# A graph network's last stages: buffers of their own for the last graph, twelve graphs fetched early, three engines for the final norm

## The reference

```
x1 = layernorm(x + attention(x, adj) @ Wo.T)               # per graph
top1 = argmax(mean_nodes(x1) @ router_w + router_b)        # one expert per graph
out = adj @ (x1 @ expert_w[top1])                          # per graph
mean, var = moments of out over all nodes of all graphs with the same expert
y = relu((out - mean) * rsqrt(var + 1e-5) * gamma[top1] + beta[top1])
result = layernorm(x1 + y)                                 # per graph
```

## Time and profile before

| | |
|---|---|
| median of 3 runs | 2607.61 us (2606.01 to 2607.66) |
| profiled execution | 2607.4 us |
| its span, first to last instruction | 2605.6 us |
| busy: PE, DVE, POOL, ACT | 86%, 69%, 65%, 60% of the span |
| granted TensorE clock, mean | 0.935 of full speed |
| chain that ended last | PE 69%, DVE 14% of the span |
| HBM read, written | 272.25 MB, 67.11 MB |

### The profile page before, as it was taken

One profiled execution on the slowest core, in us unless ns is written; L12 is line 12 of the kernel. 1 busy time (PEld: TensorE's weight loads), 2 busy tenths in 40 slices (PEclk: granted clock), 3 DMA queues, 4 the chain that ended last, 5 costly groups with the idle time before them and its releaser, 6 DMA issues.

```text
span 2605.6 us, 49110 instructions
## 1 busy us (share of the span) xinstructions
PE 2246.6 (86%) x14496; PEld 1732.1 (66%) x14496; DVE 1794.4 (69%) x4607; ACT 1563.0 (60%) x3664; POOL 1700.6 (65%) x3148
## 2 busy tenths in 40 slices
PE   3678898999989898989999898989899998986442
PEld 2456676777767676767777676767677776765332
DVE  2475867767676868677776768586777767674588
ACT  0457666666666666666666666666666666662232
POOL 0678777777777777777777777777777776771000
PEclk7789999999999999999999999999999999998766
DMA  6487474655646474746565564747465564622697
GB/s 216 137 260 236 122 250 123 195 170 183 185 149 199 138 236 128 246 118 197 168 184 181 154 197 136 238 129 245 119 204 161 185 184 153 193 82 97 232 345 246
DMA packets 215346, 476.82 MB, mean 183 GB/s; under 512 B 40944, under 2 KB 49136, under 8 KB 208304
## 3 DMA queue, kind: packets, MB, share of 16 engines
q1 hardware_dynamic: 215088, 473.74, 59.1%
HBM read 272.25 MB, written 67.11 MB: 130 GB/s over the span
## 4 chain that ended last, share of the span: by engine, by line
PE 69%; DVE 14%; issue 5%; POOL 3%; ACT 3%; SPq 3%; DMA 2%; DVEq 0%; ACTq 0%; POOLq 0%
PE t_bank L346 14%; PE p_bank L259 13%; PE p_bank L260 12%; PE p_bank L261 12%; PE o_bank L365 9%; PE s_bank L329 7%; SPq L699 2%; DVE att L493 2%; DVE ln_raw L1051 2%; POOL fold L672 2%; DVE xt L556 1%; DVE x_lo L556 1%; POOL fold L674 1%; PE o_bank L356 1%; ACT att L419 1%
## 5 line engine op out<-in xcount | busy, mean ns | idle before, releaser
L672 POOL TENSOR_TENSOR fold<-att 128x256 f32<-128x256 f32 x1024 | 765.6, 748 | 494.3 <-DVE nmax L493 407.9
L493 DVE CUSTOM_DVE_ANT_0 att<-s_bank,adj_t 128x512 f32<-128x512 f32 x1024 | 695.1, 683 | 383.1 <-PE s_bank L329 382.1
L419 ACT ACTIVATE att<-att,nmax 128x512 f32<-128x512 f32 x1024 | 738.7, 722 | 181.6 <-POOL fold L672 167.7
L467 ACT ACTIVATE pt<-t_bank 128x512 f32<-128x512 f32 x768 | 452.7, 596 | 399.1 <-PE o_bank L365 267.6
L346 PE MATMUL t_bank<-ident,att 128*128 128x128 f32 x4096 | 637.3, 279 | 19.8 <-DVE pt L502 9.5
L346 PEld LDWEIGHTS t_bank<-ident,att 128*128 128x128 f32 x4096 | 506.7, 143 | 206.1 <-issue 76.8
L329 PE MATMUL s_bank<-k_stack,q_stack 128*128 128x512 f32 x1024 | 501.4, 491 | 74.3 <-DVE nmax L493 73.8
L674 POOL TENSOR_TENSOR fold<-fold 128x128 f32<-128x128 f32 x1024 | 499.3, 488 | 80.3
L679 POOL TENSOR_TENSOR fold<-fold 128x64 f32<-128x64 f32 x1024 | 357.3, 349 | 80.2
L329 PEld LDWEIGHTS s_bank<-k_stack,q_stack 128*128 128x128 f32 x1024 | 200.0, 195 | 94.3 <-DVE nmax L493 91.6
L365 PE MATMUL o_bank<-pt,v 128*32 128x256 f32 x4096 | 248.5, 383 | 6.6 <-issue 5.8
(11 more groups left out here) (157 smaller groups left out, 3656.8 us busy)
## 6 DMA issues: line engine op xcount, KB each, us to landing
q_stack<-qk_t SPq DMA_DIRECT2D x1024, 64.0 KB, 3.2
k_stack<-qk_t SPq DMA_DIRECT2D x1024, 64.0 KB, 2.0
qk_w<-qk_split SPq DMA_DIRECT2D x123, 512.0 KB, 4.9
slot_a<-vo_split SPq DMA_DIRECT2D x16, 2048.0 KB, 9.7
slot_a<-expert_split SPq DMA_DIRECT2D x16, 2048.0 KB, 8.1
slot_b<-vo_split SPq DMA_DIRECT2D x15, 2048.0 KB, 8.2
stage<-in_xT SPq DMA_DIRECT2D x16, 1024.0 KB, 5.6
adj_t<-in_adj SPq DMA_DIRECT2D x64, 256.0 KB, 7.7
```

The costliest lines, as they stand in the source:

```text
L419: eng.activation(att[:, u % 4, j, :], att[:, u % 4, j, :], ACT.Exp, bias=nmax[:, u % 4, j:j + 1], scale=-1.0, accum_out=rsum[:, u % 4, j:j ...
L467: eng.activation(pt[:, j, :, (u % 2) * P:(u % 2 + 1) * P], t_bank[r % 2][:, :].rearrange("p (m n) -> p m n", m=NT), ACT.Copy).then_inc(act ...
L493: eng.tensor_tensor_reduce(out=att[:, u % 4, j, :], in0=s_bank[r % 2][:, :], in1=adj_t[:, t, :], scale=-2.0, scalar=3.0e38, op0=ALU.add, o ...
L672: eng.tensor_tensor(fold1[:, :], a[:, 0:256], a[:, 256:512], ALU.add).then_inc(pool_fold1, 1)
```

## The change

Four things, all at the end of the program.

1. SBUF tensors get plain views over the same bytes (`overlaid`), so that every large buffer can be the home of a graph in the last phase.
2. The second layer of graph 15 in TAIL has homes of its own: Wo in q_stack, adjT in xt, x in adj_t, the low half in v. Its loads move into the stage before (slots 10 and 13); ACT rounds adjT in slot 13 and POOL subtracts in slot 14 there. `O-` and `S-` write s_bank and t_bank, four banks. The store of x1 of graph 15 and that of its mixed result go away: both stay in SBUF. Newton's steps become ACT's Sqrt and a reciprocal.
3. The batch norm of all experts is done at once on wide tiles; the count per expert moves behind the router's choice.
4. The last phase has no loop: graph 15 first, then 0 to 14. Graphs 0 to 11 are fetched as buffers come free from slot 9 of graph 15's stage on, 12 to 14 between the stores. POOL applies scale and shift of channels 2 and 3, ACT those of 0 and 1 with relu; DVE's add also takes the maximum with 0 and sums the row; ACT squares the deviations and sums them; DVE normalises three tiles and POOL the fourth.

In the order of the pieces: the banks, `dve_rstd`, SP's two new parts, POOL's two functions of the last phase, ACT's, and DVE's adds before and after.

```diff
+        def bank_at(b, task):
+            if b == B and task[0] in ("O-", "S-"):
+                return (s_bank + t_bank)[task[1]]
+            return p_bank[bank_of[task]]
...
+            if b == B:
+                eng.wait_ge(act_std, 2)
+                eng.reciprocal(ln_rstd, ln_std).then_inc(dve_newton, 1)
...
+        def sp_last(eng, b, u):
+            if u == 9:
...
+                fetch(eng, 0)
+            if u == 10:
+                wait(eng, dve_mean, b, 1, 0)
+                wait(eng, pool_at, b, NT, 0)
+                eng.dma_start(stage[:, :, :], adjT[b].rearrange("(t p) n -> p t n", p=P)).then_inc(ld_at, 16)
+            if u == 13:
+                wait(eng, pe["score"], b, STEPS, STEPS)
+                eng.dma_start(q_stack[:].bitcast(F32), vo_dram[1]).then_inc(ld_wo, 16)
+                wait(eng, dve_logit, b, STEPS, STEPS)
+                eng.dma_start(adj_t[:, :, :], x[b].rearrange("(t p) n -> p t n", p=P)).then_inc(ld_x, 16)
+                fetch(eng, 1)
...
+            if u == 14:
+                wait(eng, pe["S"], b, NT, 0)
+                fetch(eng, 2)
+        def sp_tail(eng, b, u):
+            if u == 0:
+                wait(eng, pe["turn"], b, STEPS, 0)
+                fetch(eng, 3)
+                fetch(eng, 4)
+                wait(eng, pe["pv"], b, PAIRS, 0)
+                fetch(eng, 5)
+            if u == 5:
+                wait(eng, pe["O"], b, NT, 0)
+                fetch(eng, 6)
+                fetch(eng, 7)
...
+            def affine(n):
...
+                for t in POOL_CHANNELS:
+                    pool.tensor_scalar(y_home[i][:, t, :], y_home[i][:, t, :], g_affine[:, i, t, 0:1],
+                                       g_affine[:, i, t, 1:2], ALU.mult, ALU.add).then_inc(pool_affine, 1)
+            def normed(n):
+                z = z_home[OUT_ORDER[n]]
+                pool.wait_ge(dve_frstd, n + 1)
+                for t in POOL_ROWS:
+                    pool.tensor_scalar(z[:, t, :], z[:, t, :], f_mean[:, n % 2, t:t + 1], f_rstd[:, n % 2, t:t + 1],
+                                       ALU.add, ALU.mult).then_inc(pool_out, 1)
+            for n in range(B):
+                if n + 2 < B:
+                    affine(n + 2)
+                normed(n)
...
+            def deviation(n):
...
+                for t in range(NT):
+                    act.activation(y_home[i][:, t, :], z_home[i][:, t, :], ACT.Square, bias=f_mean[:, n % 2, t:t + 1],
+                                   accum_out=f_var[:, n % 2, t:t + 1]).then_inc(act_square, 1)
...
-                        dve.tensor_tensor(z[:, t, :], back_bank[(NT * i + t) % 8][:, :], z[:, t, :],
-                                          ALU.add).then_inc(dve_res, 1)
...
-                        dve.bn_stats(ln_raw[:, t, :], z[:, t, :]).then_inc(dve_fln, 1)
...
-                        dve.bn_aggr(ln_mv[:, t, :], ln_raw[:, t, :]).then_inc(dve_fln, 1)
...
+                    dve.scalar_tensor_tensor(out=z[:, t, :], in0=back_bank[(NT * n + t) % 8][:, :], scalar=0.0,
+                                             in1=z[:, t, :], op0=ALU.max, op1=ALU.add,
+                                             accum_out=f_sum[:, n % 2, t:t + 1]).then_inc(dve_res, 1)
...
+            residual(0)
+            for n in range(B):
+                if n + 1 < B:
+                    residual(n + 1)
+                normed(n)
```

More of the change, by code:

```diff
@@ L441, in act_slot @@
             for j in range(HG):
+                if (u, j) == (2, 0) and not attends:
+                    wait(eng, dve_newton, b, 13, -13)
+                    eng.activation(ln_std[:, 0:1], eps_c[:, :], ACT.Sqrt, bias=eps_c[:, :]).then_inc(act_std, 1)
+                if (u, j) == (6, 2) and not attends:
+                    eng.wait_ge(act_std, 1)
+                    wait(eng, dve_ln, b, 8, 0)
+                    eng.activation(ln_std, ln_mv[:, :, 1], ACT.Sqrt, bias=eps_c[:, :]).then_inc(act_std, 1)
                 if u == 7 and has_prev:
@@ L680, in pool_slot @@
                                       ALU.add).then_inc(pool_fold2, 1)
-                if u in (2, 3) and j % 2 == 1 and has_prev:
+                if u == 14 and attends and not has_next:
+                    wait(eng, act_at, b, NT, j + 1)
+                    eng.tensor_tensor(xt[:, 1, j, :], stage[:, j, :], xt[:, 0, j, :].bitcast(F32),
+                                      ALU.subtract).then_inc(pool_at, 1)
+                if u in (2, 3) and j % 2 == 1 and has_prev and attends:
                     t = 2 * (u - 2) + j // 2
@@ L739, in sp_slot @@
                 stack(eng, b, 1, 3)
-            if u == 7 and has_prev:
+            if u == 0 and not attends:
+                wait(eng, pool_at, b, NT, 0)
+                eng.dma_start(stage[0:E, 0, :], router_w).then_inc(ld_rw, 16)
+            if u == 7 and has_prev and attends:
                 wait(eng, dve_x1, b, NT, 0)
@@ L1001, in _ @@
             dve.wait_ge(dve_bn, BN_OPS * B)
-            dve.wait_ge(dve_choice, B)
-            sums, squares = bn_s[:, 0], bn_s[:, 1]
-            mean, variance = bn_mv[:, :, :, 0], bn_mv[:, :, :, 1]
-            link(dve.tensor_scalar(sums, mean, float(N), None, ALU.mult))
-            link(dve.tensor_tensor(squares, mean, mean, ALU.mult))
-            link(dve.tensor_tensor(squares, squares, variance, ALU.add))
-            link(dve.tensor_scalar(squares, squares, float(N), None, ALU.mult))
@@ new lines, in normed @@
+            def normed(n):
+                z = z_home[OUT_ORDER[n]]
+                dve.wait_ge(act_fstd, n + 1)
+                dve.reciprocal(f_rstd[:, n % 2, :], f_std[:, n % 2, :]).then_inc(dve_frstd, 1)
+                dve.wait_ge(dve_frstd, n + 1)
+                for t in range(NT):
+                    if t not in POOL_ROWS:
+                        dve.tensor_scalar(z[:, t, :], z[:, t, :], f_mean[:, n % 2, t:t + 1],
+                                          f_rstd[:, n % 2, t:t + 1], ALU.add, ALU.mult).then_inc(dve_out, 1)
```

407 lines of the change are left out of this document (235 added, 172 removed).

## The result

The kernel before took 2607.64 us (2606.01 to 2609.95, 4 runs), the changed kernel 2519.82 us (2517.74 to 2521.6, 4 runs): the ratio is 0.9667, with a 95% interval of 0.9655 to 0.9678. The profiled execution took 2520.1 us (span 2518.3). The forecast of 2530 is 10 us too high, the time lies inside the range, and the direction is right.

A forecast was written before the change was run, and what follows sets the result against it. DVE was taken to bound the last phase, with PE waiting for loads and chains before it. Gains of 14.8 - 0.3 + 9.3 + 53.1 = 76.9 us from 2607.4 gave 2530.5, stated as 2530, range 2514 to 2547.

The forecast's parts named there:

- the turn of the last phase: DVE's time per graph in the last phase, forecast at 5.8 us, with 14 such turns making 81.2 us.
- a turn under 5.2 us: Sign for the new profile: a last-phase turn this short would mean the DVE and POOL collision was priced wrong.
- Three tensor_scalars with collisions: DVE's three normalising passes per last-phase graph, alternating with POOL's passes: 2.6 us instead of 1.4 alone.
- Four adds: DVE's four adding and summing passes per last-phase graph, at 0.69 us each: 2.8 us.
- the 0.3 us charged to the attention: Loss in graph 15's attention for four added ACT copies and four POOL subtractions in slots 13 and 14: 0.3 us.
- From sum- to M-: Last graph's second layer: expert's load issued 10.0 us after sum-, 7.8 us to land, so 17.8 us instead of 21.4.
- M- to the last bn_aggr: End of the last graph's second layer, forecast to stay at 12.7 us, ending at 2421.0.
- The batch norm: From last bn_aggr to first relu: 13 instructions and ACT's root, 5.4 us instead of 14.8, gaining 9.3.
- POOL and DVE hardly meet: Rival for the last phase: turn 4.7 us, bound by DVE and ACT alike, 15 less, 2515 us; chance 17%.
- A pass costs 1.29: Rival for the last phase: POOL's pass as dear as its subtraction, turn 6.7 us, 13 more, 2543 us; chance 15%.
- the fetches are in the way: Rival for the second layer: queue at 300 GB/s instead of 389, expert's load 9 us late, 2540 us; chance 13%.
- slower: Rival for the last phase: POOL's pass of another kind, at 5 us a turn of 15.6, some 2667 us; chance 2%.

The follow-up runs named there:

- e5: Changed kernel with channel 1 moved from ACT to POOL in the last phase: 2519.63 us, ratio 0.9669 to the kernel before.
- e9: Changed kernel with the last phase's arithmetic as before (add, bn_stats, bn_aggr, four rows on DVE, POOL idle): 2580.75 us, ratio 0.9903 to the kernel before.
- e2: Changed kernel with nothing on POOL in the last phase, ACT scaling four channels and DVE normalising four tiles: 2533.36 us (one run).
- e3: Changed kernel with POOL's row pass waiting for DVE's three normalised tiles instead of DVE's reciprocal: 2513.5 us, ratio 0.9643 to the kernel before.
- e6: Changed kernel with graphs 3 to 11 fetched only when the last graph's M- is done: 2532.99 us, ratio 0.9718 to the kernel before.
- e1: Changed kernel with POOL's row given back to DVE, POOL keeping two channels and its wait for DVE's reciprocal: 2525.46 us, ratio 0.9691 to the kernel before.
- e8: Changed kernel with Wo and the second x loaded at the start of the last graph's tail: 2522.34 us, ratio 0.9674 to the kernel before.
- e4: Changed kernel with POOL's row pass waiting for DVE's three tiles and channel 1 moved to POOL: 2517.36 us, ratio 0.9663 to the kernel before.
- e7: Changed kernel with O- and S- of the last graph on two banks as before, not four: 2521.92 us, ratio 0.9673 to the kernel before.

## Why the forecast was right, and where it was off

**Bound and mechanism.** DVE bounded the last phase and still does (e5); dropping bn_stats and bn_aggr is most of the gain (e9 against e2); DVE and POOL exclude each other as the earlier trace rows hinted at 299.46 (e3); with graphs fetched early the loads are no bound, and without that they are (e6). All of that held.

**The step that was mis-sized is the turn of the last phase**: 5.8 us forecast, 5.05 measured, 14 x 0.75 = 10.5 us; the profiled time was forecast 10.4 too high (2530.5 against 2520.1), with the other terms below nearly cancelling (the last phase gave 11.6 more than forecast, the second layer 0.9 and the batch norm 0.3 less). The prediction's own sign of it came true: a turn under 5.2 us was to mean that the collision was priced wrong. Its parts:

- Three tensor_scalars with collisions: 2.6, measured 2.22. The step laid whole POOL passes (0.85) between DVE's, which makes a meeting cost 0.6; it costs 0.42. The pass alone is 0.77. Two meetings were drawn and two happen; the 0.1 taken off for one that might miss was not needed.
- Four adds 2.8, measured 2.55 with the handover to the mean. The accumulator's read (0.08) starts together with the next add, and the pitch is 0.61, not 0.69.
- Mean and reciprocal 0.5, measured 0.28: the root was done on ACT meanwhile, and the second starts before the first's record ends.

**The rest of the phase.** First mean 6.2 us after the first relu (forecast 6.7), second 9.2 (10.1), last store 5.6 after the last mean (5.7).

**The second layer.** x1's normalisation came at 2385.77 (forecast 2386.95) and sum- at 2389.41 (2390.5); 0.7 of that is an ot that was ready earlier, which says nothing, since it differs by up to 4 us between executions. So whether the 0.3 us charged to the attention were lost can't be told. Then two errors went the other way. From sum- to M- it is 18.6 us, not 17.8: the expert's load was issued 10.7 us behind sum-, not 10.0. And M- to the last bn_aggr is 14.3 us, not 12.7, as TensorE started at its lower level behind the wait that I had forecast myself. I had charged that for O-, where it did not occur (its first matmul took 0.47, not the 0.76 of the earlier trace rows), and not for M-, where it did.

**The batch norm.** 5.8 us, forecast 5.4. The product in line 1155, one of whose operands is read in another order than it is stored, took 1.08, not 0.72; the other three passes of 512 took 0.69. The gain of 9.0 was read from the two traces only; the old chain was not tried by itself in the new kernel.

**The rivals.** "POOL and DVE hardly meet" (2515) gave the nearer number at 4.7 us a turn, but its mechanism is refuted: they meet twice per turn. e3 is the kernel in which it holds, and there ACT bounds a turn of 4.56, with DVE's own at 4.21, and the time is 2513.5. "A pass costs 1.29", "the fetches are in the way" and "slower" did not occur: a pass 0.77, M- at 2408.0 with no late expert.

## What to carry to other kernels

When two engines exclude each other, price a meeting by the part that excludes (here 0.42 us of a pass of 0.77), count the meetings, and then order the other engine's passes under instructions that they don't disturb: one changed wait gave 6.4 us. Look at what the shortest instruction on the path meets before giving the helper more work. When an edit is to free an engine from a wait, look for the wait in the code that is left: e1's expectation failed there. And where a pause on TensorE is forecast that is as long as M-'s, charge slower matmuls behind it in the same step (1.7 us here).

## What the runs showed of the hardware

- A tensor_scalar of 128x512 fp32 with two per-partition operands: 0.54 us on DVE alone (0.46 from one to the next), 0.77 on POOL alone; alternating, 0.93 per pair. The two engines' passes held each other up whether they worked on one buffer (the changed kernel's row) or on two (e1).
- A DVE instruction on 4 elements per partition took 0.67 instead of 0.17 and ended with POOL's pass; an adding pass from PSUM with an accumulator took 0.68 with or without POOL beside it.
- Waits of 2.6 us (M-), 4.6 us (O- in e8) and 6.1 us (sum-) were followed by matmuls at the lower granted clock (0.52, 0.50 and 0.50 over the next 3 us), 0.43 us apart instead of 0.23; one of 1.95 us (O-) was not (1.00).
- The time at which the last attention is done differed by up to 4 us between profiled executions of kernels that differ little up to there (ot whole between 2369.9 in e4 and 2373.9 in e8). That is as much as e7 and e8 were to show, and why they are read from ot on.
